# A vision-transformer layer on one core: embedding by 98 tiles of 128 patches, v by halves, and the mixture's experts two by two

## The chip, the cores and the metric

The kernel runs on one core of one Trainium2 chip, as one program. The metric is the device time of that core in microseconds (us); lower is better. TensorE is called PE, VectorE DVE, ScalarE ACT, GpSimd POOL, and the queue that issues most transfers SP.

## What is computed

64 images of 3x224x224 are cut into 196 patches of 768 pixels each. A linear layer makes 192 features of each patch, a class token is put in front (197 tokens per image), an attention layer with 12 heads of 16 features is added (with layer norms on q and k), and then a mixture layer: 8 experts, of which each token takes two out of the best two of four groups, and one shared expert.

```python
h = _L0_tok_ref(x, W_lin, b_lin, cls_token)        # patches @ W_lin.T + b_lin, class token first
h = h + _L0_attn_ref(_layernorm(h), qkv_weight, proj_weight)
h = h + _L0_ffn_ref(_layernorm(h), gate_weight, gate_bias, w1, w2, w3, sw1, sw2, sw3)
# attention: q, k = layer_norm(q) * SCALE, layer_norm(k); softmax(q k) v; @ proj
# mixture: y = sum over experts e of cw[t, e] * (silu(x w1[e]) * (x w3[e])) @ w2[e], plus the shared expert
```

Each fp32 matrix product is made of fp16 products: an operand is split into a high and a low fp16 part, and hi x hi, hi x lo and lo x hi are added up in PSUM.

## The kernel before

**Phase A** does embedding and attention, one image per step, in a software pipeline of five stages: in step k image k is split and its embedding begins, n1 = k-1 is embedded and normalised, n2 = k-2 gets q, k and v, n3 = k-3 its scores, n4 = k-4 the rest of its attention, n5 = k-5 its projection and residual. Every engine has a function `step(k)` that writes out by hand in which order it does the pieces of the five images; an engine executes its list strictly in that order and waits on semaphores between.

An image is 2x99 slots: 98 patches, then 98 patches and the class token. Its embedding is 36 products (2 token halves x 6 chunks of 128 pixels x 3 split products), each with 99 columns of weights and 192 moved columns, done on PE in three parts of 12: `embed(n1, 1)`, `embed(n1, 2)` and, near the step's end, `embed(k, 0)`. The result of an image stands in one PSUM bank `ps_hid` (99 x 384); DVE's `hidden` (L736) adds the bias and writes `h`. The values v (`values`, 10 products, L333 to L337 into `ps_hid`) go to the same bank and DVE's `v_copy` (L796) takes them out. SP loads `xin` (fp32) and POOL loads `x_hi` (converted to fp16 by the transfer); DVE's `split` (L724) makes `x_lo`.

PE's order in a step, with the names used below:

1. attend(n4, 1); x transposes of n2; transpose_qk(n3, 0, 1); **slot a**: embed(n1, 1)
2. transpose_qk(n3, 1, 0); qk(n2, 0); transpose_qk(n3, 1, 1); **slot b**: embed(n1, 2)
3. scores(n3, 0); o transposes of n5; attend(n4, 2); qk(n2, 1); project(n5)
4. scores(n3, 1); attend(n3, 0); o_by_token(n4, 0); values(n2); transpose_qk(n2, 0, 0)
5. scores(n3, 2); **slot c**: embed(k, 0); o_by_token(n4, 1)

The order of the other engines around it: DVE does o_out(n5, 1), kT_copy(n3, 0) (L787), xT_out(n2) (L764), split, kT_copy(n3, 1), qk_variance and qk_normalise(n2, 0), hidden(n1), onT_out(n5), statistics of n1, residual(n5) (L825, waits for project), qk_variance(n2, 1) (L769), first half of norm_hidden(n1), o_out(n4, 0), qk_normalise(n2, 1), v_copy(n2), second half of norm_hidden(n1), split. ACT does, after the second square of n2: h_rstds(n1), qk_rstds(n2, 1) (L576, L579, wait for qk_variance(n2, 1)), exponent(n3, 1, 0) (L605), oT_copy(n3, 0) (L595), exponent(n3, 1, 1) (L605), qT_copy(n2, 0), and at the head of the next step exponent(n3, 2, .). scores(n3, 2) waits for both halves of exponent(n3, 1, .).

**Phase B** is the mixture: 25 groups of 512 tokens (the last of 320), each with 9 experts, on groups of four times 128 tokens. For each expert PE makes 8 products over 128 rows and 512 columns (L1263 to L1266) and then two over 64 rows (L1270): the last 64 of the 192 features need a half array only, so the product for w1 uses rows 0 to 63 and the one for w3 rows 64 to 127, side by side. Then ACT does silu (L1314), DVE the multiplication (L1345), ACT the high half (L1322), POOL the low half (L1407), PE the 12 outer products (L1284 to L1286) of the expert two before, and DVE adds them to `acc` (L1363 four times, or L1369 twice for the shared expert). Into the gaps DVE fits `route` (the gate's ranking, in six parts, L1115 to L1159) and the statistics of groups ahead. `ps_y` is two banks, one for each half of the tokens of an expert; the gate has a bank of its own.

Of the kernel before, what the change touches and what calls it, by code (L numbers as in the profile page):

```python
# [48 lines left out]
REST = (TOTAL - FULL * GT) // LANES  # L49

# [55 lines left out]
def vit_layer(nc, xp, w_lin, bias_cls, w_qkv, w_proj, w_gate, gate_bias, w13, w2,  # L106
              ident, before4, before8, out):
    hidden_dram = nc.dram_tensor("hidden_dram", [IMAGES, TOKENS, C], F32).ap()
    with ExitStack() as ctx:
# [7 lines left out]
        with ExitStack() as passing:  # L117
# [16 lines left out]
            biascls = sb("biascls", [TR, 2, C])  # L134
# [17 lines left out]
            consts_a = [(id32, ident), (biascls, bias_cls)]  # L152
            consts_b = [(gbias, gate_bias), (bef4, before4), (bef8, before8)]

            xin = [sa(f"xin{p}", [128, PCHUNKS, SLOTS]) for p in range(3)]
            x_hi = [sa(f"x_hi{p}", [128, PCHUNKS, SLOTS], F16) for p in range(3)]
            x_lo = [sa(f"x_lo{p}", [128, PCHUNKS, SLOTS], F16) for p in range(2)]
# [30 lines left out]
def phase_a(nc, xp, hidden_dram, sem, rows, bufs):  # L188
# [10 lines left out]
    (lin_hi, lin_lo, x_hi, x_lo, qkv_hi, qkv_lo, proj_hi, proj_lo, id32, biascls, eps, eps_qk, xin,  # L199
     h, stats, meanvar, h_rstd, h_lnvar, xnorm, xT_hi, xT_lo, qk_sq, qk_var, qk_lnvar, qk_rstd,  # L200
     qk_norm, qk_strips, id16, qT, kT, v, prob, oT, o_rden, o_norm, onT_hi, onT_lo, h2) = (
        bufs[n] for n in (
            "lin_hi lin_lo x_hi x_lo qkv_hi qkv_lo proj_hi proj_lo id32 biascls eps eps_qk xin "
            "h stats meanvar h_rstd h_lnvar xnorm xT_hi xT_lo qk_sq qk_var qk_lnvar qk_rstd "
            "qk_norm qk_strips id16 qT kT v prob oT o_rden o_norm onT_hi onT_lo h2").split())
    with ExitStack() as ctx:  # L206
# [9 lines left out]
        hid = ps_hid[0:TR, 0:2 * C].rearrange("p (t c) -> p t c", t=2)  # L216
# [26 lines left out]
        x_in = [sem(f"x_in{p}") for p in range(3)]  # L243
        xhi_in = [sem(f"xhi_in{p}") for p in range(3)]
# [3 lines left out]
        hid_done, xT_done, qk_done, v_done = sem("hid_done"), sem("xT_done"), sem("qk_done"), sem("v_done")  # L248
# [30 lines left out]
        def _(sp):  # L279
            def load(n):  # L280
                q = n.mod(3)

                if reached(n.times(2, -4)):
                    sp.wait_ge(xlo_done, n.times(2, -4))
                sp.dma_start(xin[q][:], xp[n.times(1)]).then_inc(x_in[q], 16)
# [13 lines left out]
            def step(k):  # L299
                if k.c == 2:  # L300
                    for n in (W_13, W_2, W_GATE):
                        load_weight(n)
                    for tile, dram in consts_b:
                        sp.dma_start(tile[:], dram).then_inc(consts_b_loaded, 16)
                if k.back(5).active():
                    store(k.back(5))
                if k.back(-3).active():
                    load(k.back(-3))
# [7 lines left out]

            load_weight(W_LIN)
            load(Index(0, 0))
# [3 lines left out]
            load(Index(0, 1))  # L322
            load_weight(W_PROJ)
            load(Index(0, 2))
# [5 lines left out]
        def _(pe):  # L330
# [8 lines left out]
            def embed(n, part):  # L339

                hi, lo = x_hi[n.mod(3)], x_lo[n.mod(2)]
                if part == 0:
                    pe.wait_ge(xlo_done, n.times(2, 2))
                    if n.c == 0:
                        pe.wait_ge(lin_split, 1)
                    if reached(n.times(1)):
                        pe.wait_ge(h_done, n.times(1))

                    if reached(n.times(1, -1)):
                        pe.wait_ge(v_set, n.times(1, -1))  # L350
                for j in range(4 * part, 4 * part + 4):
                    t, k = j // PCHUNKS, j % PCHUNKS
                    s = slice(t * TR, (t + 1) * TR)
                    pe.matmul(hid[:, t, :], hi[:, k, s], lin_hi[:, k, :], start=(k == 0), stop=False)  # L354
                    pe.matmul(hid[:, t, :], hi[:, k, s], lin_lo[:, k, :], start=False, stop=False)  # L355
                    last = pe.matmul(hid[:, t, :], lo[:, k, s], lin_hi[:, k, :], start=False,  # L356
                                     stop=(k == PCHUNKS - 1))
                if part == 2:
                    last.then_inc(hid_done, 1)
# [1111 lines left out]
```

## Time and profile before

| | us |
|---|---|
| median of 2 runs (lowest to highest) | 1674.95 (1672.44 to 1677.46) |
| the profiled execution: its time | 1680.21 |
| its span, first to last instruction | 1678.0 |
| PE busy | 1611.4 (96%) |
| DVE busy | 1275.9 (76%) |
| ACT busy | 987.5 (59%) |
| POOL busy | 676.0 (40%) |

Phase A runs from the start to about 947 us, phase B from about 953 us to the end. A timeline row gives the start in us, the duration in us, the engine, the line of the kernel, the operation, what it writes and reads, and how many instructions were merged in the row; in square brackets stands the idle time of the engine before it and who ended it. Matmuls overlap: the time that one costs is the distance between two starts and not its duration. The same holds to a small degree for DVE and ACT, where a start can lie some 0.1 us ahead of the end of the one before.

### The profile page before, as it was taken

The numbers are of one execution on the slowest core, as the hardware profiler recorded it, in microseconds if no ns is written. First come the engines' busy times: TensorE is split into PE (matmuls) and PEld (weight loads), VectorE is DVE, ScalarE is ACT, GpSimd is POOL, SyncE is SP. The second block draws the span as 40 slices with busy tenths as digits, with TensorE's granted clock in tenths as the row PEclk, the third lists the DMA queues.
The fourth block names the chain that finished last, engine by engine and source line by source line (L and its number), as shares of the span: only waits on it lengthen the run. The fifth ranks groups of instructions, "written<-read, shape, count | busy, mean of one in ns | idle before, by whom it ended". The sixth has DMA issues, their size and how long they took to land. (4 is left out here: it accounts for less than half of the span.)

```text
span 1678.0 us, 44146 instructions
## 1 busy us (share of the span) xinstructions
PE 1611.4 (96%) x16714; PEld 1104.3 (66%) x16714; DVE 1275.9 (76%) x3610; ACT 987.5 (59%) x2038; POOL 676.0 (40%) x758
## 2 busy tenths in 40 slices
PE   4999999999999999999998799999999999999998
PEld 4777777777777777777776455555555555555555
DVE  5787777777777777777775488888888878888877
ACT  2777777777777777777766344454545454444543
POOL 2333333333333333333332155554545545555543
PEclk8999999999999999999998599999999999999999
DMA  7233333333333333333310111112121211111110
GB/s 242 69 78 78 78 78 78 78 78 78 78 78 78 78 78 78 78 78 78 106 42 19 30 42 40 56 39 57 36 61 33 58 39 45 52 42 55 34 35 16
DMA packets 97695, 108.11 MB, mean 64 GB/s; under 512 B 61323, under 2 KB 74286, under 8 KB 97358
## 3 DMA queue, kind: packets, MB, share of 16 engines
q1 hardware_dynamic: 88270, 85.83, 17.3%
q0 software_dynamic: 9216, 19.47, 7.6%
q8 instruction: 134, 2.20, 0.5%
q14 instruction: 75, 0.61, 0.1%
HBM read 92.44 MB, written 19.37 MB: 67 GB/s over the span
## 5 line engine op out<-in xcount | busy, mean ns | idle before, releaser
L1407 POOL TENSOR_TENSOR in_lo<-inner,in_hi 128x512 f16<-128x512 f32 (+1 forms) x225 | 259.2, 1152 | 354.5 <-ACT act L1314 342.0
L919 POOL CAST qk_strips<-qk_norm 99x768 f16<-99x768 f32 x128 | 104.9, 820 | 583.6 <-DVE qk_norm L776 583.6
L605 ACT ACTIVATE prob<-ps_sc 99x792 f32<-99x792 f32 x384 | 303.7, 828 | 6.2 <-PE ps_sc L416 2.8
L1322 ACT ACTIVATE in_hi<-inner 128x512 f16<-128x512 f32 (+1 forms) x225 | 140.3, 623 | 198.3 <-DVE inner L1345 198.3
L1363 DVE SCALAR_TENSOR_TENSOR acc<-ps_y,comb,acc 128x192 f32<-128x192 f32 (+1 forms) x700 | 242.0, 408 | 0.3 <-PE ps_y L1286 0.3
L1314 ACT ACTIVATE act<-ps_h 128x512 f32<-128x512 f32 (+1 forms) x225 | 132.0, 587 | 182.0 <-PE ps_h L1270 182.0
L1345 DVE SCALAR_TENSOR_TENSOR inner<-ps_h,act 128x512 f32<-128x512 f32 (+1 forms) x225 | 152.9, 680 | 113.0 <-ACT act L1314 110.6
L1284 PE MATMUL ps_y<-w_hi,in_hi 128*128 128x192 f16 (+1 forms) x900 | 224.2, 249 | 3.1 <-DVE acc L1363 2.8
L1286 PE MATMUL ps_y<-w_hi,in_lo 128*128 128x192 f16 (+1 forms) x900 | 221.4, 246 | 0.0
L1285 PE MATMUL ps_y<-w_lo,in_hi 128*128 128x192 f16 (+1 forms) x900 | 221.4, 246 | 0.0
L354 PE MATMUL ps_hid<-lin_hi,x_hi 128*99 128x192 f16 x768 | 194.1, 253 | 18.8 <-DVE x_lo L724 10.5
L356 PE MATMUL ps_hid<-lin_hi,x_lo 128*99 128x192 f16 x768 | 191.2, 249 | 0.0
L355 PE MATMUL ps_hid<-lin_lo,x_hi 128*99 128x192 f16 x768 | 191.1, 249 | 0.0
L1263 PE MATMUL ps_h<-yT_hi,w_hi 128*128 128x512 f16 (+1 forms) x450 | 169.7, 377 | 7.7 <-PEq L206 7.7
L431 PE MATMUL ps_o<-prob,v 98*32 98x198 f32 (+1 forms) x3072 | 171.5, 341 | 0.0
L921 POOL TENSOR_TENSOR qk_strips<-qk_norm,qk_strips 99x384 f16<-99x384 f32 x128 | 165.7, 1295 | 10.6
L1264 PE MATMUL ps_h<-yT_lo,w_hi 128*128 128x512 f16 (+1 forms) x450 | 169.7, 377 | 0.0
L1266 PE MATMUL ps_h<-yT_hi,w_hi 128*128 128x512 f16 (+1 forms) x450 | 169.6, 377 | 0.0
L1265 PE MATMUL ps_h<-yT_hi,w_lo 128*128 128x512 f16 (+1 forms) x450 | 169.6, 377 | 0.0
L787 DVE COPY kT<-ps_mix 128x594 f16<-128x594 f16 x128 | 60.5, 473 | 97.4 <-PE ps_mix L400 96.7
L416 PE MATMUL ps_sc<-qT,kT 64*99 64x198 f16 x1536 | 106.3, 257 | 20.6 <-ACT prob L605 19.2
L1284 PEld LDWEIGHTS ps_y<-w_hi,in_hi 128*128 128x128 f16 (+1 forms) x900 | 88.2, 98 | 56.4 <-issue 45.9
(167 smaller groups left out, 3818.0 us busy)
## 6 DMA issues: line engine op xcount, KB each, us to landing
xin<-xp SPq DMA_DIRECT2D x64, 594.0 KB, 4.3
x_hi<-xp POOLq DMA_DIRECT2D x64, 297.0 KB, 4.0
hidden_dram<-h SPq DMA_DIRECT2D x64, 147.0 KB
hin<-hidden_dram SPq DMA_DIRECT2D x24, 384.0 KB, 3.4
out<-acc SPq DMA_DIRECT2D x24, 384.0 KB, 2.7
w_f<-w SPq DMA_DIRECT2D x1, 2304.0 KB, 9.1
yT_hi<-y_hi SPq DMA_TRANSPOSE x100, 2.4
yT_lo<-y_lo SPq DMA_TRANSPOSE x100, 2.4
```

The costliest lines, as they stand in the source:

```text
L354: pe.matmul(hid[:, t, :], hi[:, k, s], lin_hi[:, k, :], start=(k == 0), stop=False)
L355: pe.matmul(hid[:, t, :], hi[:, k, s], lin_lo[:, k, :], start=False, stop=False)
L356: last = pe.matmul(hid[:, t, :], lo[:, k, s], lin_hi[:, k, :], start=False, stop=(k == PCHUNKS - 1))
L431: last = pe.matmul(o_quad[VB * place:VB * place + VB, :], v[p][rows, m, QUAD * quad + place, :], prob[quad][rows, place, m, :], start=(m = ...
L605: act.activation(prob[quad][:, places].rearrange("p h m s -> p h (m s)"), ps_sc[0:TR, places, 0:2 * SLOTS], ACT.Exp, scale=D ** -0.5 / (SQ ...
L1263: pe.matmul(bank, w13_hi[:, 0, e, w, :], y_hi[:, 0], start=True, stop=False)
L1264: pe.matmul(bank, w13_hi[:, 0, e, w, :], y_lo[:, 0], start=False, stop=False)
L1284: pe.matmul(dst, in_hi[b][:, s], w2_hi[:, e, :], start=True, stop=False)
L1285: pe.matmul(dst, in_hi[b][:, s], w2_lo[:, e, :], start=False, stop=False)
L1286: last = pe.matmul(dst, in_lo[b][:, s], w2_hi[:, e, :], start=False, stop=True)
L1363: last = dve.scalar_tensor_tensor(out=acc[p][0:R, t, :], in0=ps_y[half_no][0:R, u * C:(u + 1) * C], scalar=comb[p][0:R, t, e:e + 1], in1=b ...
L1407: pool.tensor_tensor(in_lo[b][:, 0:N], inner[b][:, 0:N], in_hi[b][:, 0:N], ALU.subtract).then_inc(inlo_done, 1)
```

## The change

**Embedding.** The patches of all images are taken as one row of 12544, in 98 tiles of 128 (`TILES`). A tile is 18 products with 128 columns of weights, done as two halves of 9 (chunks 0 to 2, chunks 3 to 5); a half is counted as u, tile j = u // 2. `halves_of(step)` gives three halves to each step (four in steps 14, 31 and 46), and `slots_of` lays one in slot a, one in slot b and the rest in slot c. `ps_hid` holds one tile (128 x 192). DVE's `hidden` evacuates a tile to `h_rows`, and SP moves the rows from there by DMA (SBUF to SBUF, `place`, two or three transfers per tile) to the slots in `h` where attention has always had them; the class token rows are written once by 8 small transfers. The statistics of an image wait for these transfers (`h_in`). Inputs have four buffers in place of three and are split three halves ahead, in three DVE instructions per step in place of two.

**v by halves.** v goes to columns 198 to 389 of the bank `ps_o`, whose first 198 columns hold the attention output of a quad. `values(n2, 0)` stands where values(n2) stood, `values(n2, 1)` behind scores(n3, 2), and DVE copies each half out by itself.

**Mixture.** Experts are taken in pairs through all 225 (`two_by_two`): 16 full products, then the gate where it is due, then the four 64-row products, then the 24 outer products of the pair before. `inner`, `in_hi`, `in_lo` have four buffers in place of three, `ps_y` four banks in place of two, and the gate writes into the free columns of one of them. DVE does two multiplications, then the sums of the pair before, then the parts of `route` and the statistics that fall to the two experts.

The core of the diff:

```diff
-            def embed(n, part):
+            def embed(us):
+                for u in us:
+                    if u is None:
+                        continue
+                    j, half_no = u // 2, u % 2
+                    pe.wait_ge(xlo_done, u + 1)
+                    if half_no == 0 and j > 0:
+                        pe.wait_ge(h_done, j)
+                    for k in range(3 * half_no, 3 * half_no + 3):
+                        pe.matmul(hid, x_hi[j % 4][:, k, :], lin_hi[:, k, :], start=(k == 0), stop=False)
...
+            def values(n, t, attended):
+                if t == 0 and attended.active():
+                    pe.wait_ge(oT_out, attended.times(QUADS, 1))
+                if reached(n.times(2, t)):
+                    pe.wait_ge(v_set, n.times(2, t))
+                from_xT(v_ps, t, slice(2 * C, 3 * C)).then_inc(v_done, 1)
...
@@ PE step
                 if n4.active():
                     o_by_token(n4, 0, n5, n2)
                 if n2.active():
-                    values(n2, n1)
+                    values(n2, 0, n3)
                     if n4.active():
                         pe.wait_ge(onorm_done, n4.times(2, 1))
                     transpose_qk(n2, 0, 0)
                 if n3.active():
                     scores(n3, 2)
-                if k.active():
-                    embed(k, 0)
+                if n2.active():
+                    values(n2, 1, n3)
+                embed(c)
@@ DVE step
+                hidden(slots_of(k.c - 1)[2] if k.c > 0 else (1,))
                 if n3.active():
                     kT_copy(n3, 0)
                 if n2.active():
                     xT_out(n2)
-                if k.active():
-                    split(k, 1)
+                split(ahead[0])
                 if n3.active():
                     kT_copy(n3, 1)
+                hidden(a)
                 if n2.active():
                     qk_variance(n2, 0)
                 if n2.active():
                     qk_normalise(n2, 0)
-                if n1.active():
-                    hidden(n1)
+                hidden(b)
...
                 if n5.active():
                     residual(n5)
+                split(ahead[1])
                 if n2.active():
                     qk_variance(n2, 1)
...
+                    v_copy(n2, 0)
                     qk_normalise(n2, 1)
-                    v_copy(n2)
+                    v_copy(n2, 1)
@@ SP
+            def place(u):
+                if u is None or u % 2 == 0:
+                    return
+                j = u // 2
+                sp.wait_ge(h_done, j + 1)
+                for n, t, row, to, rows_here in pieces_of(j):
+                    if n >= HB:
+                        sp.wait_ge(h2_done, n - HB + 1)
+                    sp.dma_start(h[n % HB][to:to + rows_here, t, :],
+                                 h_rows[j % 4][row:row + rows_here, :]).then_inc(h_in[n % HB], 16)
@@ mixture, PE
+            def turn(own, older_products):
+                for g, e in own:
                     inner_products(g, e)
...
+                for g, e in own:
+                    inner_tails(g, e)
+                for following in scored:
+                    pe.wait_ge(tanh_done, following.times(1, 1))
+                older_products()
+            two_by_two(turn, outer_products)
@@ mixture, DVE
+            def turn(own, older_sums):
+                for g, e in own:
                     multiply(g, e)
+                older_sums()
+                for g, e in own:
...
+                    if e == 0:
+                        rows.route(dve, g, 5)
                     if e in (1, 2) and ahead.active():
                         rows.stats_of(dve, ahead, e - 1)
-                    if e in (4, 5, 6) and following.active():
+                    if e > 3 and following.active():
                         rows.route(dve, following, e - 4)
```

## Rows read from the trace of the kernel before

**Rows 1.** Busy time by stretch, phase A and phase B: busy us (instructions) by engine, clock, DMA.

```profile
300.00:400.00 100.00, 97.73 (x1267) 75.88 (x1266) 73.12 (x195) 70.13 (x151) 35.86 (x38) 1.00 0.34 79
1100.00:1200.00 100.00, 100.00 (x767) 57.48 (x766) 83.76 (x255) 47.45 (x91) 49.53 (x56) 1.00 0.19 53
```

**Rows 2.** Timeline of PE in one step of phase A.

```profile
500.26 0.44 PE L400 MATMUL ps_mix<-id,qk_strips 99*128 99x99 f16 x6
500.54 0.25 PE L354 MATMUL ps_hid<-lin_hi,x_hi 128*99 128x192 f16 x1
...
505.17 0.55 PE L416 MATMUL ps_sc<-qT,kT 64*99 64x198 f16 x8
...
506.86 0.25 PE L333 MATMUL ps_hid<-qkv_hi,xT_hi 128*99 128x192 f16 x1
...
508.61 0.55 PE L416 MATMUL ps_sc<-qT,kT 64*99 64x198 f16 x8 [0.30 <-ACT prob L605]
509.09 0.29 PE L354 MATMUL ps_hid<-lin_hi,x_hi 128*99 128x192 f16 x1
...
513.28 0.33 PE L333 MATMUL ps_qk<-qkv_hi,xT_hi 128*99 128x384 f16 x1
```

**Rows 3.** Timeline of DVE in the same step.

```profile
500.74 0.47 DVE L787 COPY kT<-ps_mix 128x594 f16<-128x594 f16 x1 [0.83 <-PE ps_mix L400]
...
503.72 0.61 DVE L743 BATCH_NORM_STATS2 stats<-h 99x6 f32<-99x192 f32 x2
...
505.27 0.56 DVE L825 SCALAR_TENSOR_TENSOR h<-ps_mix,h 99x384 f32<-99x384 f32 x1 [0.55 <-PE ps_mix L337]
505.75 0.54 DVE L769 TENSOR_REDUCE qk_var<-qk_sq 99x24 f32<-99x384 f32 x1
...
512.61 0.56 DVE L764 SCALAR_TENSOR_TENSOR xT_lo<-ps_qk,xT_hi 128x396 f16<-128x396 f32 x1
```

**Rows 4.** Timeline of ACT in the same step.

```profile
506.80 0.81 ACT L605 ACTIVATE prob<-ps_sc 99x792 f32<-99x792 f32 x1
507.51 0.33 ACT L595 ACTIVATE oT<-ps_o 128x198 f32<-128x198 f32 x1
507.73 0.83 ACT L605 ACTIVATE prob<-ps_sc 99x792 f32<-99x792 f32 x1
```

**Rows 5.** Timeline of PE around the 64-row products of one expert of phase B.

```profile
1245.42 0.38 PE L1263 MATMUL ps_h<-yT_hi,w_hi 128*128 128x512 f16 x1
...
1246.93 0.38 PE L1266 MATMUL ps_h<-yT_hi,w_hi 128*128 128x512 f16 x1
1247.24 0.39 PE L1270 MATMUL ps_h<-yT_lo,w_lo 64*128 64x512 f16 x2
1247.57 0.26 PE L1284 MATMUL ps_y<-w_hi,in_hi 128*128 128x192 f16 x1
...
1248.57 0.38 PE L1263 MATMUL ps_h<-yT_hi,w_hi 128*128 128x512 f16 x1
```

**Rows 6.** Page, part 6: transfers: queue, count, KB each, us from issue to landing.

```profile
xin<-xp SPq DMA_DIRECT2D x64, 594.0 KB, 4.3
```

**Rows 7.** Page, part 5: a group's busy us, mean ns of one, idle before it.

```profile
L1284 PEld LDWEIGHTS ps_y<-w_hi,in_hi 128*128 128x128 f16 (+1 forms) x900 | 88.2, 98 | 56.4 <-issue 45.9
```

**Rows 8.** Timeline of DVE over two experts of phase B.

```profile
1243.87 0.61 DVE L1115 TENSOR_TENSOR cmp<-masked 128x256 f32<-128x256 f32 x1
...
1245.54 0.69 DVE L1345 SCALAR_TENSOR_TENSOR inner<-ps_h,act 128x512 f32<-128x512 f32 x1
1246.15 1.38 DVE L1363 SCALAR_TENSOR_TENSOR acc<-ps_y,comb,acc 128x192 f32<-128x192 f32 x4
1247.45 0.41 DVE L1124 TENSOR_TENSOR cmp<-cmp,eq 128x256 f32<-128x256 f32 x1
...
1248.37 0.69 DVE L1345 SCALAR_TENSOR_TENSOR inner<-ps_h,act 128x512 f32<-128x512 f32 x1
```

**Rows 9.** Timeline of PE where the pipeline of phase A runs empty.

```profile
903.97 0.53 PE L333 MATMUL ps_qk<-qkv_hi,xT_hi 128*99 128x384 f16 x1 [1.03 <-ACT xT_hi L557]
```

More of the change, by code:

```diff
@@ L242, in phase_a, with halves_of, slots_of, pieces_of @@
         FIRST_PIECE = 6
-        x_in = [sem(f"x_in{p}") for p in range(3)]
-        xhi_in = [sem(f"xhi_in{p}") for p in range(3)]
+        x_in = [sem(f"x_in{p}") for p in range(4)]
+        xhi_in = [sem(f"xhi_in{p}") for p in range(4)]
+        h_in = [sem(f"h_in_a{q}") for q in range(HB)]
+        half_done = sem("half_done")
+        def halves_of(step):
+            first = AHEAD + 3 * step + sum(step > e for e in EXTRA)
+            count = 4 if step in EXTRA else 3
+            return [u for u in range(first, first + count) if u < 2 * TILES]
+        def slots_of(step):
+            us = halves_of(step) + [None] * 4
+            return us[0:1], us[1:2], us[2:4]
+        def pieces_of(tile):
+            found = []
+            for m in range(128 * tile // HALF, (128 * tile + 127) // HALF + 1):
+                lo, hi = max(HALF * m, 128 * tile), min(HALF * m + HALF, 128 * tile + 128)
+                found.append((m // 2, m % 2, lo - 128 * tile, lo - HALF * m, hi - lo))
+            return found
+        arrivals = [1 + n // HB for n in range(IMAGES)]
+        for j in range(TILES):
+            for n, t, row, place, rows_here in pieces_of(j):
+                for later in range(n, IMAGES, HB):
+                    arrivals[later] += 1
+        for n in range(IMAGES):
+            arrivals[n] -= n // HB
         xlo_done = sem("xlo_done")
         h2_out = rows.h2_out
-        hid_done, xT_done, qk_done, v_done = sem("hid_done"), sem("xT_done"), sem("qk_done"), sem("v_done")
+        xT_done, qk_done, v_done = sem("xT_done"), sem("qk_done"), sem("v_done")
         qkT_done, sc_done, av_done = sem("qkT_done"), sem("sc_done"), sem("av_done")
@@ L304, in step @@
                         sp.dma_start(tile[:], dram).then_inc(consts_b_loaded, 16)
+                a, b, c = slots_of(k.c)
+                if k.c == 0:
+                    place(1)
+                else:
+                    for u in slots_of(k.c - 1)[2]:
+                        place(u)
+                for j in range(loaded(k.c - 1), loaded(k.c)):
+                    load(j)
+                place(a[0])
+                place(b[0])
                 if k.back(5).active():
                     store(k.back(5))
-                if k.back(-3).active():
-                    load(k.back(-3))
                 if k.c == IMAGES - 6:
@@ L315, in step, with loaded @@
                     rows.transposes(sp, b_group(0), k.c - IMAGES - 1)
+            def loaded(step):
+                return 4 if step < 0 else min(TILES, 6 + 3 * step // 2 + step // 32)
             load_weight(W_LIN)
-            load(Index(0, 0))
+            load(0)
             load_weight(W_QKV)
@@ L321, in _ @@
                 sp.dma_start(tile[:], dram).then_inc(consts_a_loaded, 16)
-            load(Index(0, 1))
+            load(1)
             load_weight(W_PROJ)
-            load(Index(0, 2))
+            for q in range(HB):
+                sp.dma_start(h[q][TR - 1:TR, :, :], cls_rows).then_inc(h_in[q], 16)
+            load(2)
+            load(3)
             run(step)
@@ L887, in _ @@
             remainder(lin_lo[:], lin_hi[:], lin_f[:]).then_inc(lin_split, 1)
-            split(Index(0, 0), 0)
+            for u in range(AHEAD + 3):
+                split(u)
             run(step)
```

289 lines of the change are left out of this document (143 added, 146 removed).

## The prediction

> **What bounds the kernel now.** I read the busy time by stretch first. PE is busy 97.73 of 100 us in phase A and all of 100 in phase B, where DVE has 73.12 and 83.76 [rows 1]. So PE sets the time, and a product taken away pays, as long as PE doesn't come to wait for something instead. Whether it does is not in the shares but in the order of one step, so I read the timelines of PE, DVE and ACT over one image [rows 2 to 4] and over two experts [rows 5, 8]. An image has 176 matmuls (36 embedding, 20 q and k, 10 v, 10 projection, 24 scores, 48 attention, 24 + 8 + 6 transposes); 1267 in 100 us [rows 1] make 13.89 us per image. An expert costs 3.15 us: its first full product starts at 1245.42, that of the next at 1248.57 [rows 5].
>
> One chain of phase A matters most. residual (L825) starts 0.10 us after scores(n3, 1), because it waits for project; qk_variance follows 0.48 later [rows 3], the first half of exponent(n3, 1) 1.05 after that, oT_copy(n3, 0) 0.71 later, the second half 0.22 later and for 0.83 us [rows 4]; only then may scores(n3, 2) start, at 508.61 against 505.17, 3.44 us after scores(n3, 1) [rows 2]. PE fills these 3.44 us with its own list but for the 0.30 that the row of 508.61 shows. The chain has no slack: whatever is put into it comes out at PE.
>
> **The embedding.** 64 x 36 = 2304 products become 98 x 18 = 1764. A product with 192 columns costs 0.083 us (twelve in 1.00 us, with 128 columns of weights [rows 5]), so 540 products are 45 us, 0.70 us per image, 0.25 in each of the slots a, b and c. What becomes of each:
>
> Slot a: the next thing but a transpose is qk(n2, 0), at 513.28 [rows 2], and it waits for xT_lo, which starts at 512.61 and takes 0.56 [rows 3]: ready at 513.17. Of the 0.25 us only about 0.06 is gained.
>
> Slot b: where it does not wait it gives 0.25. But `ps_hid` holds one tile, and a tile is two halves, so an even half waits for DVE's hidden of the tile before. With three halves per step, slot a ends a tile in every second step (call it step A) and slot b begins the next. hidden(a) is queued on DVE behind kT_copy(n3, 1), and that waits for the transposes which PE does right ahead of slot b. Transposes at 500.26, kT_copy at 500.74 for 0.47 [rows 2, 3], less the 0.08 by which DVE's instructions overlap (0.56 long, 0.48 apart at 505.27), then hidden at about 501.13. Four sums of its width, 192, take 1.30 us [rows 8], so it costs 0.33 and with its overlap ends at 501.54. PE goes on there instead of at 500.54 [rows 2]: 1.00 lost, 0.25 gained, so 0.75 dearer in step A. In the other steps (B) slot b ends a tile, and slot c, far behind, begins the next without a wait. The hidden of slot c is ready before the next slot a by a margin of some 0.1 us.
>
> Slot c gives 0.25; the three steps with a fourth half give back 0.03 on average.
>
> **v by halves.** values(n2, 0) now waits for oT_copy(n3, 0), since both live in `ps_o`. Before, v started at 506.86, while oT_copy ran from 507.51 to 507.84 [rows 2, 4]: PE would stand from 506.86 to 507.89 even with nothing else changed. And split(ahead[1]) is put between residual and qk_variance, that is into the chain. It is 384 wide like residual, so 0.48 [rows 3]. values(n2, 0) then starts 0.10 + 0.48 + 0.48 + 1.05 + 0.71 + 0.33 + 0.04 = 3.19 us after scores(n3, 1), and scores(n3, 2) at 0.10 + 0.48 + 0.48 + 1.05 + 0.71 + 0.22 + 0.83 + 0.05 = 3.92 [rows 3, 4]; the last terms, 0.04 and 0.05, are the way from an end to PE's start (508.56 to 508.61). PE's own way is as long: 3.19, five products 0.44, transposes 0.28 [rows 2], 3.91. So the middle of a step grows from 3.44 to 3.92: +0.48. The other half of v, which used to lie inside the chain, now lies behind scores(n3, 2) with nothing to cover: +0.41. What the middle loses in PE work it gains nothing from, because the chain ends last.
>
> DVE also gets a third split, a second v_copy and one and a half evacuations in place of one, all together 0.1 to 0.2 us per step of fixed parts. v_copy(n2, 1) comes late, and the second half of norm_hidden, the split of slot c and o_out(n5, 1) stand behind it; transpose_qk(n3, 0, 1) waits for the last. I take 0.08 per step; the bounds are 0 (it stays inside DVE's 27% idle [rows 1]) and 0.3.
>
> Sum per step: A -0.06 + 0.75 + 0.48 + 0.41 - 0.25 = +1.33; B -0.06 - 0.25 + 0.48 + 0.41 - 0.25 = +0.33; mean 0.83, with 0.03 and 0.08 some 0.94 us. Over the 62 steps that hold all five stages: +58 us.
>
> **Rows by DMA.** A tile is some 2.3 transfers on SP's queue. SP waits for h_done ahead of each and the x loads and the store of h2 stand behind; they have a step of lead. The tightest case is a tile ended in slot c: its hidden runs at the head of the next step, ahead of kT_copy(n3, 0), so it ends by 512.2, or 498.3 in the step shown, and the statistics start at 503.72 [rows 3], 5.4 us later. No transfer of this kind is in the trace. The nearest takes 4.3 us for 594 KB [rows 6], and the rows of a tile are 96 KB; with up to 1.1 for three issues that is hidden just so. I take nothing. The other end: the rows lie behind an x load too (now 384 KB, 2.8 by size), 2.8 us late in every second step, +80 us.
> Start and end of the phase, with eight small transfers more, one latency more and the same chain in the steps without embedding: +3 us (0 to 8).
>
> **The mixture.** From the last full product to the first outer one is 0.64 us, from 1246.93 to 1247.57; a full product is 0.216 (seven in 1.51) and the two 64-row ones together as much, so 0.21 us are lost on going over to half rows and back [rows 5]. Done once for two experts, this saves 0.21 us per pair: 112 pairs, 23 us; the other end is nothing. The scores are 64-row products that alternate between the row halves too: eight take 0.48 us from 508.61 to 509.09 [rows 2], where one after the other eight of 198 columns would take 0.68, so four in a row do pack.
>
> The Trainium skill, TensorE: Matmul & The Clock Gate, "The mechanism" under packing, says that a weight load overlaps a running matmul only when it goes to other rows of the array. A load takes 98 ns [rows 7]; by that rule the third product, on the rows of the first, would expose it, 0.10 us per pair, and 12 of the 23 us would be left. The eight scores speak against it.
>
> Can DVE follow? A pair lasts 6.09 us. Two multiplications are 2 x 0.61, eight sums 2 x 1.30 [rows 8]; 2.27 us are left. The dearest parts that fall into one turn are the two of the 8x8 ranking: 1.67 and 0.92 us [rows 8], 2.59 together, 0.32 too much. But the first multiplication has slack: it starts 1.13 after the 64-row products and takes 0.69 [rows 5, 8], 1.82, and its bank is wanted again only 2 x 0.22 + 0.11 + 24 x 0.083 = 2.54 after them. 0.7 of slack covers 0.32, and the turn after has less to do. So PE stays the bound. The gate's wait for the tanh is hidden by four 64-row products (0.54).
>
> **Sum.** 58 + 3 - 23 = +38 us. On the profiled execution's span of 1678.0, 1716, with 2.2 around it 1718; that execution lies 5 us above the median, so against the median 1675 the forecast is **1713 us**.
>
> **Rivals.**
>
> *Both waits are absorbed* (faster): the chain has slack that I don't see, or DVE does hidden(a) early; PE pays for its products alone: -45 - 23, 1607 us. For it speaks that PE is the busy engine [rows 1]; against it the two starts, 506.86 against 507.84, and DVE's written order. It decides if values(n2, 0) waits under 0.3 us. Chance 0.12.
>
> *One wait only*: the middle is as I say, but slot b doesn't wait in steps A (or the other way round): mean step +0.44, 27 us, + 3 - 23: 1682. Chance 0.15.
>
> *PE's clock falls in phase A.* Where the pipeline runs empty, a product of qk takes 0.53 us right after an idle time of 1.03 [rows 9], against 0.33 at 2.4 GHz [rows 2]: that is 1.2 GHz. After the change PE idles for about 1.4 us in the middle and 1 us at slot b of steps A. If a fifth of phase A ran at 1.2 GHz, with half of it hidden in the waits, +45 us, 1758; at more, over 1790. Against it: a step would still hold 12.8 of 14.8 us of work. Chance 0.07.
>
> The Trainium skill, TensorE: Matmul & The Clock Gate, "PE-mode transpose", says that transposes don't count as activity for the clock; this would make the middle of a step, where o_by_token and transpose_qk stand around the wait, look idler than it is. No row here separates it.
>
> *Phase B saves nothing or DVE becomes its bound*: 1736 without the 23 us; with 0.2 us per pair lost on top 1759. For it: DVE's 83.76 becomes 87 when a pair takes 6.09 instead of 6.30. Chance 0.07.
>
> *The rows come late*, as priced above: 1793. For it: a margin of under 1 us. Against it: slot c's rows are issued ahead of that step's x loads. Chance 0.04.
>
> **How the numbers follow.** My forecast, with its own range of 1690 to 1738, has 0.55. The range 1662 to 1768 takes in the case of one wait, most of phase B's and of the clock's and leaves out the faster one, a badly fallen clock and late rows. A measurement of this kernel tells about 2%, 33.5 us, from no change. Faster by over 2% is the first rival: 0.12. Slower means over 1708.4: 0.6 of my forecast, and the last three rivals: 0.51. The rest, 0.37, is within 2%.
>
> **What would show it.** Right: a step of phase A of about 14.8 us, alternately 15.2 and 14.2; the first v product waiting over 1 us for oT (L595's successor) in every step; the first product of slot b waiting about 1 us for hidden in every second; a pair of experts at about 6.1 us with PE at 100%. Wrong: PE at 97% or more in phase A (then the waits were absorbed), statistics that wait for the row transfers, clock under 1.00 between 100 and 850 us, or multiplications that PE waits for in phase B.

## The result and the profile after

The changed kernel takes 1786.53 us (median of 1782.13 and 1790.92) against 1674.95: ratio 1.067, 95% interval 1.053 to 1.080. The forecast was 1713, range 1662 to 1768: the direction was right, the size was not, and the time lies outside the range. The profiled execution took 1782.13 with a span of 1780.2, 102.2 more than the span of before. The stretches below are taken from the starts of the same instructions in both traces:

| stretch | before | after | measured | forecast |
|---|---|---|---|---|
| start to the first residual | 70.2 | 84.3 | +14.0 | +3 with the end |
| first to last residual (63 steps) | 876.2 | 957.7 | +81.5 | +58 |
| last residual to phase B's first full product | 6.9 | 9.9 | +3.0 | in the 3 |
| phase B, from there to the end of the span | 724.7 | 728.3 | +3.6 | -23 |

Between the two profiled executions the miss is therefore 64 us (a span of 1780.2 where 1716 was forecast; between the medians it is 73.5). It has three parts: 27 in phase B, 23.5 in the steps, 14 at the two ends. Busy time by stretch (us, busy time with instructions of PE, PEld, DVE, ACT, POOL, clock, DMA), a stretch of each phase. They are to be held against [rows 1]:

```profile
300.00:400.00 100.00, 86.62 (x1091) 65.00 (x1088) 69.90 (x198) 63.29 (x137) 27.30 (x36) 1.00 0.33 80
1200.00:1300.00 100.00, 95.70 (x760) 57.23 (x758) 88.11 (x250) 46.20 (x91) 47.88 (x56) 1.00 0.18 49
```

PE fell from 97.73 to 86.62 and from 100 to 95.70: it is no longer the engine that sets the time, the waits are. DVE is busier in phase B (83.76 to 88.11) though it starts fewer instructions (255 to 250 in 100 us). The clock stands at 1.00. The next lines are PE's waits over 300 to 500 us (13 steps), then over 1150 to 1550 us (14 groups of experts): total us, times, longest.

```profile
PE ps_o L394 <- ACT oT L656: 17.4, 13, 1.3
PE ps_hid L412 <- DVE h_rows L802: 5.7, 6, 1.0
PE ps_mix L458 <- DVE o_norm L873: 4.2, 13, 0.3
...
PE ps_h L1345 <- DVE inner L1442: 10.2, 13, 1.0
PE ps_y L1155 <- issue: 2.5, 7, 1.0
```

The first two are the waits of the forecast, 1.3 us in each step and 1.0 in every second. The third was priced at 0.08 and the fourth at nothing. The fifth stands ahead of the gate's products; the trace links it to nothing, and the forecast had the gate's wait hidden. The timeline of PE over one step, to be held against [rows 2]:

```profile
507.75 0.55 PE L474 MATMUL ps_sc<-qT,kT 64*99 64x198 f16 x8
...
510.94 0.29 PE L394 MATMUL ps_o<-qkv_hi,xT_hi 128*99 128x192 f16 x1 [1.34 <-ACT oT L656]
...
511.76 0.55 PE L474 MATMUL ps_sc<-qT,kT 64*99 64x198 f16 x8
...
515.54 0.44 PE L458 MATMUL ps_mix<-id,qk_strips 99*128 99x99 f16 x6 [0.32 <-DVE o_norm L873]
...
519.24 0.24 PE L412 MATMUL ps_hid<-lin_hi,x_hi 128*128 128x192 f16 x1 [0.92 <-DVE h_rows L802]
```

v starts 3.19 us behind scores(n3, 1), to the hundredth the forecast, scores(n3, 2) 4.01 instead of 3.92. No wait stands ahead of scores(n3, 2): the exponent ends 3.86 behind scores(n3, 1), and PE's own five products and transposes take 0.82 where 0.72 was reckoned, so PE's own way ends last here, by 0.10. Two of DVE's rows and two of POOL's show what stands ahead of the 0.32:

```profile
509.55 0.31 DVE L825 TENSOR_SCALAR xnorm<-h,meanvar,h_rstd 99x64 f32<-99x64 f32 x1
...
513.45 0.91 DVE L825 TENSOR_SCALAR xnorm<-h,meanvar,h_rstd 99x64 f32<-99x64 f32 x1
...
512.49 0.82 POOL L989 CAST qk_strips<-qk_norm 99x768 f16<-99x768 f32 x1 [4.91 <-DVE qk_norm L842]
513.39 0.92 POOL L991 TENSOR_TENSOR qk_strips<-qk_norm,qk_strips 99x384 f16<-99x384 f32 x1
```

The same instruction takes 0.31 us where POOL does nothing and 0.91 where POOL's L991 has begun 0.06 us earlier; both end together, at 514.36 and 514.31. It is not the only thing ahead of the 0.32: DVE also stood idle for 0.47 us at 512.89, for the second half of v that PE now makes behind scores(n3, 2). Phase B shows it larger. First come rows of PE (the first two from an earlier turn, in which nothing is late), then DVE and then POOL over one turn of two experts:

```profile
1187.08 0.60 PE L1357 MATMUL ps_h<-yT_lo,w_lo 64*128 64x512 f16 x4
1187.62 0.26 PE L1373 MATMUL ps_y<-w_hi,in_hi 128*128 128x192 f16 x1
...
1202.74 0.39 PE L1345 MATMUL ps_h<-yT_hi,w_hi 128*128 128x512 f16 x1 [0.81 <-DVE inner L1442]
...
1198.22 0.16 DVE L1215 TENSOR_SCALAR chosen<-rank 128x16 f32<-128x16 f32 x1
1198.42 1.01 DVE L1217 TENSOR_SCALAR drop<-chosen 128x16 f32<-128x16 f32 x1
1199.46 0.86 DVE L1221 TENSOR_TENSOR masked<-biased,chosen 128x32 f32<-128x32 f32 x1
...
1201.99 1.29 DVE L1442 SCALAR_TENSOR_TENSOR inner<-ps_h,act 128x512 f32<-128x512 f32 x2
...
1198.20 1.20 POOL L1496 TENSOR_TENSOR in_lo<-inner,in_hi 128x512 f16<-128x512 f32 x1
1199.36 0.91 POOL L1142 TENSOR_TENSOR y_lo<-bnorm,y_hi 128x384 f16<-128x384 f32 x1
```

The four half-row products take 0.54 us, as forecast, and the turns that nothing disturbs last 6.08 (forecast 6.09). But `drop`, 16 elements wide, takes 1.01 and ends (1199.43) with POOL's in_lo (1199.40); `masked` takes 0.86 and ends (1200.32) with POOL's y_lo (1200.27). In the kernel before `drop` (there L1142 of route) took 0.175 on average from 1000 to 1600 us. DVE comes to its next multiplications 7.7 us after the last ones (1194.29), where a turn of PE is 6.08, and PE waits 0.81.

### The profile page after: what moved, and what is told of

It is laid out like the page before. It is cut to its first block and busy times, and to the rows that moved or that the text cites. A ratio compares the mean times of both kernels' runs of the same rounds, so it can differ in the third digit from the quotient of the medians.

```text
span 1780.2 us, 43873 instructions
## 1 busy us (share of the span) xinstructions
PE 1563.5 (88%) x16174; PEld 1062.7 (60%) x16174; DVE 1345.2 (76%) x3776; ACT 980.5 (55%) x2038; POOL 640.4 (36%) x792
## 5 line engine op out<-in xcount | busy, mean ns | idle before, releaser
L1496 POOL TENSOR_TENSOR in_lo<-inner,in_hi 128x512 f16<-128x512 f32 (+1 forms) x225 | 254.5, 1148 | 351.9 <-ACT in_hi L1412 351.9
L1404 ACT ACTIVATE act<-ps_h 128x512 f32<-128x512 f32 (+1 forms) x225 | 120.8, 588 | 227.0 <-PE ps_h L1357 223.9
L1442 DVE SCALAR_TENSOR_TENSOR inner<-ps_h,act 128x512 f32<-128x512 f32 (+1 forms) x225 | 143.1, 678 | 73.0 <-ACT act L1404 54.3
L412 PE MATMUL ps_hid<-lin_hi,x_hi 128*128 128x192 f16 x588 | 147.5, 251 | 47.6 <-DVE h_rows L802 38.0
L414 PE MATMUL ps_hid<-lin_hi,x_lo 128*128 128x192 f16 x588 | 147.6, 251 | 0.0
L413 PE MATMUL ps_hid<-lin_lo,x_hi 128*128 128x192 f16 x588 | 147.5, 251 | 0.0
L648 ACT ACTIVATE qT<-ps_mix 128x594 f16<-128x594 f16 x128 | 86.1, 672 | 106.9 <-PE ps_mix L458 106.9
L458 PE MATMUL ps_mix<-id,qk_strips 99*128 99x99 f16 x1536 | 110.7, 208 | 28.8 <-DVE o_norm L873 19.4
L787 DVE TENSOR_TENSOR x_lo<-xin,x_hi 128x384 f16<-128x384 f32 x196 | 107.7, 552 | 18.0 <-issue 12.4
L991 POOL TENSOR_TENSOR qk_strips<-qk_norm,qk_strips 99x384 f16<-99x384 f32 x128 | 117.3, 917 | 10.6
## 6 DMA issues: line engine op xcount, KB each, us to landing
h<-h_rows SPq DMA_DIRECT2D x32, 73.5 KB
```

The source lines that it names most:

```text
L1442: dve.scalar_tensor_tensor(out=inner[q][:, 0:N], in0=ps_h3[b][:, 0:N], scalar=SA / SS, in1=act1[b][:, 0:N], op0=ALU.mult, op1=ALU.mult).th ...
L1496: pool.tensor_tensor(in_lo[b][:, 0:N], inner[b][:, 0:N], in_hi[b][:, 0:N], ALU.subtract).then_inc(inlo_done, 1)
```

## The experiments

Most variants ran once, and whole times scatter by some us from one execution to the next (in one of them a lone step takes 19.7 us). So steps are compared: a step is the time from one residual to the next, numbered by the image of the first, and the stretch is 27 to 40, where no weight piece and no fourth half falls. Before, a step took 13.94. In the changed kernel it takes 15.87 in a step A and 14.80 in a step B; the forecast, laid on 13.94, gives 15.27 and 14.27. Phase B is given from its first full product to the end of PE's last: 721.3 us before, 724.5 changed.

**One phase of each.** `a_new_b_old` has the new phase A with the old phase B, `a_old_b_new` the other way round.

> Phase A of the changed kernel, phase B of the kernel before. In the two traces phase B lasts 728.3 us after and 724.7 before, where the forecast had it 23 us shorter. If the two phases don't touch each other, this kernel takes 1782 - 4 = 1778 us, and phase A still begins phase B at about 1052. If the loss of phase B came only from the late start or from what phase A leaves behind, phase B would stay at 728.

> Phase A of the kernel before, phase B by pairs. If the pairs are worth nothing because DVE comes late in some turns, 1680 + 4 = 1684 us. If the pairs bring their 23 us and the changed phase A took them away, 1657.

Measured 1786.5 (phase B 721.5) and 1678.3 (phase B 724.0, kernel before 1677.1 beside it). So all of the loss but some 3 us is phase A's, and the pairs, worth 23 us by the forecast, are worth nothing as they stand.

**The middle of the step.** `split_late`:

```diff
                     residual(n5)
-                split(ahead[1])
...
                     o_out(n4, 0)
+                split(ahead[1])
```

> The changed kernel with one edit: the second split of a step stands behind o_out(n4, 0), where DVE waits 1.08 us for v, instead of between residual and qk_variance(n2, 1). Theory of the chain: values(n2, 0) and scores(n3, 2) start 0.47 us earlier in each step, 64 x 0.47 = 30 us, 1752. Rival, DVE's sum: 1782. Rival, the split is then in the way of v_copy and moves the loss to the end of the step: between.

1754.6; steps 15.40 and 14.33, 0.47 shorter each. The split in the chain costs what an instruction 384 wide costs, 0.48.

`oT_first`:

```diff
-                    exponent(n3, 1, 0)
                     oT_copy(n3, 0)
+                    exponent(n3, 1, 0)
                     exponent(n3, 1, 1)
```

> The changed kernel with one edit: ACT does oT_copy(n3, 0) ahead of the first half of exponent(n3, 1), not behind it. values(n2, 0) waits for it and can start 0.7 us earlier. Theory of the chain: scores(n3, 2) waits for the second exponent, which starts when it did before, so PE's wait only moves from the first product of v to scores(n3, 2): 1782 within 6 us. Rival, the wait for oT is itself the price: 0.7 us less in each of 64 steps, 1737.

1766.4; steps 15.44 and 14.36, so 0.44 shorter, which lies between the two. v's wait falls from 17.4 us in 13 steps to 7.5, and scores(n3, 2) waits in its place, the second of these lines (waits of PE, 300 to 500 us):

```profile
PE ps_o L394 <- ACT oT L656: 7.5, 13, 0.6
PE ps_sc L474 <- ACT prob L666: 7.1, 13, 0.7
```

In the middle of the step the theory of the chain holds: scores(n3, 2) starts 3.91 behind scores(n3, 1), only 0.10 earlier. The other 0.34 come from the end of the step. v_copy(n2, 0) and qk_normalise(n2, 1) are done earlier, so POOL's strips are too, and the xnorm of 64 columns no longer falls beside them (rows of DVE, then of POOL):

```profile
503.67 0.63 DVE L823 TENSOR_SCALAR xnorm<-h,meanvar,h_rstd 99x192 f32<-99x192 f32 x1
504.22 0.30 DVE L825 TENSOR_SCALAR xnorm<-h,meanvar,h_rstd 99x64 f32<-99x64 f32 x1
...
503.27 0.92 POOL L991 TENSOR_TENSOR qk_strips<-qk_norm,qk_strips 99x384 f16<-99x384 f32 x1
```

The two xnorm together take 0.85 us from start to end instead of 1.20, and the wait of 0.32 is gone.

`v_in_chain` is `oT_first` with the second half of v ahead of scores(n3, 2), inside the chain again.

> As the run with oT_copy first, and PE does values(n2, 1) ahead of scores(n3, 2) instead of behind it. Theory of the chain: PE's wait for the exponent covers it, 0.41 to 0.45 us less per step, 27 us, 1755. If the second half of v has to wait for the copy of the first (DVE does o_out(n4, 0) before it), a part is lost: 1755 to 1782.

1746.4; steps 15.01 and 13.94, 0.42 less than `oT_first`. The forecast had priced that half, uncovered, at 0.41. In steps 15 to 25 a step A grew instead (15.44 to 15.69): DVE's split waits there for the load of x, which is the subject of the next two variants (8.9 us in 5 times, 300 to 425 us).

**hidden(a).** `hidden_early`:

```diff
+                hidden(a)
                 if n3.active():
                     kT_copy(n3, 1)
-                hidden(a)
```

> The changed kernel with one edit: on DVE hidden(a) stands ahead of kT_copy(n3, 1), so slot b need not wait for it. Theory of places: the steps in which slot a ends a tile become 1.0 us shorter (15.87 to 14.87), the others stay at 14.80; 32 such steps, 32 us, 1750. Rival, that phase A is bound by the sum of DVE's work: nothing changes, since DVE does the same instructions, 1782.

1764.6: only half of it. In steps 27 to 40 a step A fell from 15.87 to 14.80, the whole 1.07; in steps 15 to 25 only to 15.33. There DVE's split waits for something that the trace does not link ("issue": 3.0 us in 4 times, 300 to 425 us), and slot b waits behind it. I took it for the half-precision copy of x on POOL's queue, of which one more is loaded ahead from the kernel's step(29) on. `hidden_early_x` has that from step(12) on:

```diff
-                return min(TILES, 8 + 3 * step // 2 + (step + 3) // 32)
+                return min(TILES, 8 + 3 * step // 2 + (step + 20) // 32)
```

> hidden(a) ahead of kT_copy(n3, 1), as in the run that gave 1764.6, and the x_hi loads of POOL's queue one tile earlier from step 12 on. Theory (with hidden early the next thing that is late in steps A is the half-precision copy of x, which DVE's split waits for in all steps but those from 27 to 41, where a load more is ahead): steps A of 14.8 us everywhere behind step 11, total about 1753. Rival (the wait of the split is for something else): steps A stay at 15.3 to 15.5 outside 27 to 41, total 1762 to 1767.

1756.2, with 14.79 in every plain step from 15 to 40 and all but two of the later ones. The wait of the split is gone from the trace of that stretch. Behind the wait removed stood another, a load that came some 0.5 us earlier than hidden(a) and so did not show.

**The end of the step.** `last_split_head`:

```diff
-                for u in ahead[2:4]:
-                    split(u)
...
+                if k.c > 0:
+                    for u in [u + 3 for u in halves_of(k.c - 1)][2:4]:
+                        split(u)
                 if n3.active():
                     kT_copy(n3, 0)
```

> One edit to the changed kernel: the third split of a step moves from its end to the head of the next, ahead of kT_copy(n3, 0), where DVE is idle for 0.5 us. Theory (transpose_qk(n3, 0, 1) waits 0.3 us in every step because DVE reaches o_out(n5, 1) late, behind a split and an xnorm that POOL stretches from 0.31 to 0.91 us): each step 0.3 us shorter, 19 us, total about 1765. Rival (the 0.3 us come out again in the next wait, the chain over residual or hidden(a), which are reckoned from the step's start): total 1780 to 1788.

1774.9; steps 15.40 and 14.43: 0.47 and 0.37 shorter, the wait of 0.32 is gone. The xnorm still takes 0.91 here. This run takes the split away and `oT_first` takes the long xnorm away, and the wait goes in either: it needs both. In steps 15 to 25 a step A gained little (15.80); the late load would explain it, but no run with this edit alone and earlier loads shows it.

**The start.** `weights_late` issues the weights of the mixture in step 2 behind that step's rows.

> One edit to the changed kernel: SP issues the weights of the mixture in step 2 behind that step's row transfers and x loads, not ahead of them. Theory (the 5.96 us that the statistics wait at 42.5 us are for rows that stand behind 2.4 MB of weights in the queues): the wait goes, first residual at about 78 instead of 84, total about 1777. Rival (the rows are late for another reason, or the time is lost again to another wait of the fill): first residual at 83 to 85, total 1780 to 1788.

1778.6. The statistics no longer wait 5.96 us for rows; the first residual starts at 78.80 instead of 84.25. Steps are unchanged.

**Phase B.** `route_spread` puts parts 0 to 2 of the ranking into the turn of expert 4, part 3 into that of 6 and part 4 into that of 8.

> The changed kernel with one edit in phase B: DVE's parts of route fall to experts 4 (parts 0 to 2), 6 (part 3) and 8 (part 4), so that no turn holds both a 4x4 part and the 8x8 comparisons, or the 8x8 comparisons and the ranks. PE waits 20.4 us in all for a late multiplication and some more at the gate. If the overfull turns are the cause, phase B takes 728 - 20 to 728 - 27 = 701 to 708 and the kernel 1755 to 1762. If DVE's sum is the bound (88 of 100 us), nothing changes: 1782.

1790.2, phase B 728.4: slower. From 1150 to 1550 us PE waits 6.6 us for late multiplications instead of 10.2, but 7.8 instead of 2.5 ahead of the gate; the trace links that wait to nothing. And in the new places the parts met POOL as well; one row (cmp, 0.61 in [rows 8] and 0.42 where POOL does nothing):

```profile
1261.76 1.40 DVE L1190 TENSOR_TENSOR cmp<-masked 128x256 f32<-128x256 f32 x1
```

`all_ab` is this with all of `v_in_chain`, `split_late` and `hidden_early`.

> All edits together: hidden(a) early, split late, oT_copy first, values(n2, 1) ahead of scores(n3, 2), route spread. If the places add up, 1782 - 32 - 30 - 27 - 22 = 1671 us, and more if DVE's lateness at the end of a step (0.33 us, 21 us in all) goes too: 1650. If one bound takes over from the other, above 1690.

1717.3: steps of 13.83 at either parity from 27 to 40, but 15.04 in a step A before that, and phase B at 728.7. That pointed at the load of x and at POOL.

`pairs_rests_first` has the old phase A and moves POOL's y_lo halves, so that they don't run at the end of a turn:

```diff
+                    if e == 8 - g.c % 2 and g.back(-2).active():
+                        pool.wait_ge(mul_done, g.times(NE, e + 1))
+                        rows.rest_of(pool, g.back(-2), 0)
+                    if e == g.c % 2 and g.c > 0 and g.back(-1).active():
+                        pool.wait_ge(mul_done, g.times(NE, e + 1))
+                        rows.rest_of(pool, g.back(-1), 1)
                     inner_rest(g, e)
...
-                    if e == 6 and g.back(-2).active():
-                        rows.rest_of(pool, g.back(-2), 0)
-                    if e == 7 + g.c % 2 and g.back(-2).active():
-                        rows.rest_of(pool, g.back(-2), 1)
```

> Phase A of the kernel before, the pairs of experts, and one edit more: POOL's y_lo (two halves per group, 1.3 us each) no longer runs behind in_lo at the end of a turn, beside DVE's small instructions of the ranking, but ahead of in_lo in the next turn, beside DVE's multiplications and sums that read PSUM. Theory (DVE's instructions of the ranking took 0.65 us for 0.17, 0.54 for 0.22 because POOL held the SBUF port, 1.4 us per group, and PE lost 0.98 us per group to that): the small instructions take what they took before, PE is busy 99 to 100% in phase B, phase B lasts some 700 us instead of 724, total 1653. Rival (a turn of a pair is overfull by DVE's own work, whatever POOL does): L1140's 0.65 us may fall, but phase B stays at 718 to 724 us, total 1672 to 1678.

1793.2, phase B 839.1: neither theory came true. My place for the second half was too late for the transposes behind it, and the gate of each group waited. The busy time of a stretch, and rows of PE's timeline:

```profile
1100.00:1200.00 100.00, 89.56 (x648) 52.91 (x646) 71.93 (x218) 40.51 (x80) 42.14 (x50) 0.92 0.14 39
```

```profile
1161.52 0.17 PE L1080 MATMUL ps_y<-gate_hi,yT_hi 128*128 128x8 f16 x1 [3.61 <-issue]
...
1162.13 1.04 PE L1282 MATMUL ps_h<-yT_lo,w_lo 64*128 64x512 f16 x4
...
1170.65 0.61 PE L1282 MATMUL ps_h<-yT_lo,w_lo 64*128 64x512 f16 x4
```

With one such wait in it a group takes 33.6 us, 4.6 more than in `a_old_b_new`. Part of it is the clock: the granted clock is 0.56 from 1160 to 1164 us, that is mostly the lower level of 1.2 GHz, and 1.00 again from 1168 on. The four products at 1162.13, right behind the wait, take 1.04 us, those of the next turn 0.61.

`pairs_rests_silu` places both halves earlier, each released by the silu that opens a turn; ACT's normalise and POOL's rstds of a group move by an expert with them:

```diff
-                    if e == 5 and ahead.active():
+                    if e == 5 - g.c % 2 and ahead.active():
                         rows.normalise(act, ahead, 0)
-                    if e == 6 + g.c % 2 and ahead.active():
+                    if e == 6 and ahead.active():
@@ POOL (rstds of odd groups stand ahead of inner_rest(g, 3))
+                    if e in (6 - g.c % 2, 8 - g.c % 2) and g.back(-2).active():
+                        pool.wait_ge(silu_done, g.times(NE, e + 1))
+                        rows.rest_of(pool, g.back(-2), int(e > 6))
                     inner_rest(g, e)
```

> Phase A of the kernel before, the pairs, and POOL's y_lo halves at the start of a turn, released by the turn's first silu, each early enough for the transposes that the gate reads (in the run before the gate waited 3.6 us per group for them). Theory (the pairs bring their 0.21 us each once POOL's y_lo does not run beside DVE's small instructions): small instructions at 0.17 to 0.2 us, PE busy 99 to 100% in phase B, phase B some 700 us, total about 1653. Rival (a turn of a pair is overfull by DVE's own work): small instructions fast, and yet phase B at 715 to 724 us, total 1668 to 1678.

**1648.99 us against 1674.99, ratio 0.985 (0.983 to 0.988)**: 1.5% faster than the kernel before (medians of 4 and 7 executions). Phase B is 694.4, and from 1050 to 1450 us the trace shows no wait of PE, not at the gate either. Its stretch of phase B; then the group of `chosen` over 1000 to 1600 us (busy us, mean ns, idle before) in this kernel, and the same in `a_old_b_new`:

```profile
1200.00:1300.00 100.00, 100.00 (x790) 60.21 (x789) 86.94 (x264) 47.42 (x92) 50.70 (x59) 1.00 0.18 51
```

```profile
L1140 DVE TENSOR_SCALAR chosen<-rank 128x16 f32<-128x16 f32 x22 | 3.7, 169 | 0.4
```

```profile
L1140 DVE TENSOR_SCALAR chosen<-rank 128x16 f32<-128x16 f32 x21 | 13.5, 645 | 0.4
```

`rests_silu_alone` moves POOL's halves so in the kernel before, without the pairs.

> The kernel before with one edit: POOL's y_lo halves at the start of an expert's turn, behind its silu; no pairs. Theory (the pairs bring the 27 us, and moving y_lo only takes away what the pairs had brought with them; here PE is busy all the time anyway): phase B stays at 721 us (first product to last), total 1672 to 1680. Rival (the move of y_lo is what shortens phase B): phase B at 695 to 710 us, total 1650 to 1665.

1675.8 beside 1673.0, phase B 720.1. So the 27 us are the pairs', 4 more than forecast; the move takes away only what they had brought along. What ACT's and POOL's moved statistics give of it was not measured by itself.

**All together.** `all_fixed` has all edits of phase A with the phase B of `pairs_rests_silu`; `all_fixed_no_L` has the same but for the last split, which stays at the end of the step.

> All edits of phase A together (hidden(a) ahead of kT_copy(n3, 1), second split behind o_out(n4, 0), oT_copy(n3, 0) ahead of the first exponent, second half of v ahead of scores(n3, 2), x_hi a tile earlier, last split at the head of the next step, weights behind the rows) and the phase B of the run pairs_rests_silu. Theory (the causes add up, and the x_hi loads were what was left in steps A): a step of 13.8 us at either parity, phase A about as long as in the kernel before or 5 us longer, phase B 700 us, total about 1657. Rival (the last split at the head makes kT_copy late in short steps, or something else becomes late): steps of 14.2 to 15, total 1680 to 1710.

> The same with the last split where the changed kernel has it, at the end of a step. Theory: steps of 13.84 us at either parity, as in the all_ab run's steps 27 to 41; total about 1660. Against all_fixed it prices the last split's place in a short step: more than 0.1 us per step if DVE is late at the step's end, nothing if PE's own chain ends last there.

`all_fixed` takes 1661.63 (median of 4, ratio 0.992, 0.990 to 0.995) and `all_fixed_no_L` 1654.5 in its one execution. Steps are 13.84 at either parity in both; the weight-piece steps are 14.62 and 14.88 with the last split at the head and 14.27 and 14.55 with it at the end, so it is better left at the end once the chain is short. With all the causes found gone phase A is as long as before: in `all_fixed_no_L` the first 56 steps take 782.6 us, before 783.6, and the first residual starts at 74.9, before at 70.2. Of the 0.70 us that the products save per step 0.10 is left. In that step v, which took 1.02 us in one piece (506.86 to 507.88), takes 0.70 and 0.55 in two, starts 0.31 later behind o_by_token, and its second half waits in each step:

```profile
PE ps_o L394 <- DVE v L860: 4.1, 14, 0.3
```

v in one piece with the new tiles wasn't tried: a tile stays open in `ps_hid` over two slots, so v can't go between them there. The best version found is `pairs_rests_silu`, the old phase A with the pairs.

## Why the prediction was wrong in size

**Embedding, slots.** At slot b of steps A 1.00 lost was forecast; the row says 0.92, steps A and B differ by 1.07, and `hidden_early` gave those 1.07 back in steps 27 to 40. That was right. The products were forecast at 0.70 us per image less; the slots show that, but the waits use it up.

**v by halves.** Start of v 3.19 (forecast 3.19), split in the chain 0.47 (0.48), second half 0.42 (0.41). That was right. Scores(n3, 2) came at 4.01 instead of 3.92, 0.09 late, since PE's own products and transposes took 0.10 longer than reckoned and not the chain.

**DVE late at the end of a step.** This is the term of the sum for a step that was mis-sized: 0.08, with 0.3 as its upper bound; moving the last split away gave 0.37 to 0.47 per step. The order that makes DVE late was named rightly. But I had counted DVE's own work and taken each instruction at its length of before, and POOL's strips stood in the sum for nothing. They follow qk_normalise(n2, 1), and the xnorm of 64 columns now falls beside them and takes 0.91 for 0.31. `oT_first` shows what that is worth: without it the end of a step is 0.34 shorter and DVE is in time. Of the 0.53 by which a step B exceeds the forecast, 0.37 to 0.47 is this term and 0.09 the middle. Over the 56 steps ahead of the drain the measured excess is 85.1 us against 53 by the forecast, 32 too little. The last seven steps came out 3.6 us shorter than before where I had reckoned some 6 more, which leaves the 23.5; that part is luck, since in the five traces with the old phase A the last seven take 86.2 to 92.7 us, and 92.7 is the kernel before.

**Start and end.** +3 was forecast (0 to 8), +17 measured, 14.0 of it at the start. 5.4 of it are rows that stood behind the weights in SP's queue: the argument "the rows are hidden" was made for a plain step and held there (no wait for rows but this one), not for step 2. The other edits of `all_fixed_no_L` bring 3.9 more; some 4.7 at the start and the 3.0 at the end stay unexplained.

**Phase B.** -23 was forecast, +3.6 came. The saving was real: 0.22 us per undisturbed turn, four half-row products in 0.54. The Trainium skill, TensorE: Matmul & The Clock Gate, "The mechanism", by which the third product would expose its weight load, is not borne out: by it the turn would be 6.19, measured 6.08. The step that failed is "0.7 of slack covers 0.32". The 0.32 was reckoned with DVE's instructions as long as in the trace of before. In a pair the two in_lo and the two y_lo of POOL stand one behind the other, from 1.5 to 6.4 us behind the start of the multiplications, just where the small instructions now stand: parts 2 and 3 took 3.77 us, where at the lengths of before they are some 2.5 and in `pairs_rests_silu` 2.08, and `a_old_b_new` paid 1.4 us of DVE per group. The trace of before held the hint: [rows 8] has two instructions of 128x256 at 0.61 and 0.41, and the longer stands beside POOL. The rival "DVE becomes the bound" named the right end (1736 to 1759, had phase A been right) with the wrong mechanism and 0.07.

**The rivals.** Waits absorbed, or one of them: wrong, both are there in full. Clock: wrong, 1.00 from 100 to 850 us, though PE idles some 2 us in 15; in `pairs_rests_first` it fell behind one wait of 3.6 us. Rows late: wrong in the plain steps. The late x load that `hidden_early` uncovered was not among them; it costs nothing as long as hidden(a) is later.

**The range** held each term's own bounds but no common one. Start at 8, DVE at 0.3 per step and no gain in phase B, all within bounds that I gave singly, make 58 + 14 + 8 = 80 and 1755. Three terms passed their bounds, and two of them, the step's end and phase B, for the same unseen reason: an instruction whose length depends on what another engine does.

## What to carry to other kernels

When work is moved or bunched, don't take the durations of before as fixed: put the timelines of DVE and POOL side by side and see which small SBUF-to-SBUF instructions of the one will now stand beside the other. An instruction of 16 elements per partition took a microsecond here, and the cure was to move the other engine's work, not its own. And remove a wait together with what is late next: here hidden(a), then the x load; v's wait, then the exponent's. Each looked like half a fix alone.

## What the runs showed of the hardware

Some DVE instructions with all operands in SBUF wait for a POOL instruction that has begun and end with it: `drop` (0.175 alone) took 1.01 and `masked` (0.19 alone) 0.86 us. Those that read PSUM did not: the sums from ps_y took 0.409 us on average in `a_old_b_new` and 0.408 before. The Trainium skill, SBUF — State Buffer, "SBUF: two separate sides", describes this as an exclusive lock on a port pair that DVE and GpSimd share, held for a whole instruction; the equal ends of the rows above agree. Not every instruction with all operands in SBUF waits: the statistics of h took 0.35 us each beside POOL and 0.34 alone in the changed kernel, and x_lo in the kernel before 0.77 beside POOL (61 of them) and 0.77 alone. What tells the two kinds apart no run here shows.

The granted clock stayed at 1.00 with 1.3 and 0.9 us idle in a step of 15, and was 0.92 in a 100 us stretch of `pairs_rests_first` with one wait of 3.6 us per group of 34.
